# Interleaving softmax tiles and banded-weight reads with the normalise, write and transpose steps of a windowed-attention layer on eight cores

## What is computed

```python
xn = layernorm(x)
w = softmax(einsum('btc,fc->btf', xn, w_lin).reshape(B, T, H, K))   # 31 weights per row and head
# banded weights: row t of head h uses rows t-30 .. t of xn
out = einsum('bhts,bhsr->bhtr', banded(w), heads(xn))
x = x + out
w_ternary = where(w > d, 1, where(w < -d, -1, 0))   # d = 0.7 * mean(|weight|)
x = x + layernorm(x) @ (w_ternary * alpha).T + bias
```

## Time and profile before

| | |
|---|---|
| device time, median of 2 runs | 425.77 us (417.42 and 434.12) |
| the profiled execution, device time | 420.13 us |
| its span on the slowest core (core 7) | 418.6 us |
| spans of the eight cores | 406.2 to 418.6 us |
| busy: PE, DVE, ACT | 41%, 32%, 17% |
| mean DMA rate | 154 GB/s |

### The profile page before, as it was taken

One profiled execution on the slowest core, in us unless ns is written; L12 is line 12 of the kernel. 1 busy time (PEld: TensorE's weight loads), 2 busy tenths in 40 slices (PEclk: granted clock), 3 DMA queues, 4 the chain that ended last, 5 costly groups with the idle time before them and its releaser, 6 DMA issues.

```text
span 418.6 us, 2990 instructions; the slowest of 8 cores (406.2 to 418.6 us)
## 1 busy us (share of the span) xinstructions
PE 170.6 (41%) x940; PEld 94.6 (23%) x940; DVE 131.9 (32%) x250; ACT 69.7 (17%) x78; POOL 5.8 (1%) x8
## 2 busy tenths in 40 slices
PE   0000304000522532547579059530000499299990
PEld 0000001000200110114578059430000133033330
DVE  1462985200220220222585327460000022222321
ACT  0007045918010111011100000005650000000000
POOL 5000000000000000000000000000000000000000
PEclk9999856655656756676655555555555599689996
DMA  7999931089998996443699999602227676733422
GB/s 230 283 255 313 341 80 33 1 205 223 296 141 164 201 150 179 100 100 75 152 203 163 141 246 174 109 0 100 100 100 164 101 96 101 198 145 138 165 100 101
DMA packets 85544, 64.53 MB, mean 154 GB/s; under 512 B 69008, under 2 KB 70032, under 8 KB 85528
## 3 DMA queue, kind: packets, MB, share of 16 engines
q10 hardware_dynamic: 33136, 48.31, 43.9%
q1 hardware_dynamic: 51288, 15.01, 23.6%
q0 software_dynamic: 1104, 1.02, 1.9%
HBM read 23.14 MB, written 25.40 MB: 116 GB/s over the span
## 4 chain that ended last, share of the span: by engine, by line
DMA 33%; ACTq 14%; PE 14%; DVE 10%; ACT 9%; SPq 9%; DVEq 4%; issue 4%; POOLq 1%
DMA stage<-wpad 15%; ACTq L555 10%; SPq L199 9%; DMA wlTb<-wlT 8%; DMA wet<-stage 4%; DMA xn2d<-xn2r 3%; PE ps_at L618 3%; ACT xn L497 3%; ACT xn2r L536 2%; PE ps_ff L641 2%; PE ps_ff L643 2%; DVEq L337 2%; PE ps_wp L641 2%; PE ps_wp L643 2%; DVE redt L300 2%
## 5 line engine op out<-in xcount | busy, mean ns | idle before, releaser
L591 PE MATMUL ps_wp<-wlTb,xn1T 128*128 128x496 bf16 x128 | 45.1, 532 | 97.6 <-ACT wpad L457 85.0
L618 PE MATMUL ps_at<-wins,wet 128*64 128x64 bf16 x512 | 50.8, 305 | 28.8 <-DMA wet<-stage 21.5
L618 PEld LDWEIGHTS ps_at<-wins,wet 128*64 128x64 bf16 x512 | 50.2, 216 | 29.7 <-issue 29.7
L641 PE MATMUL ps_ff<-wtern,xn2T 128*128 128x512 bf16 x64 | 27.4, 428 | 61.7 <-DMA xn2T<-xn2d 53.7
L591 PEld LDWEIGHTS ps_wp<-wlTb,xn1T 128*128 128x128 bf16 x128 | 16.1, 131 | 126.1 <-issue 123.0
L335 DVE TENSOR_REDUCE sumc<-wpad 128x16 f32<-128x496 bf16 x16 | 10.7, 666 | 84.7 <-ACT wpad L457 84.7
L382 DVE TENSOR_TENSOR outst<-ps_ff,xs 128x512 f32<-128x512 f32 x16 | 10.3, 686 | 72.4 <-PE ps_ff L645 55.6
L345 DVE TENSOR_TENSOR xs<-ps_at,xs 128x1024 f32<-128x1024 f32 x16 | 19.6, 1223 | 29.3 <-PE ps_at L618 29.3
L643 PE MATMUL ps_ff<-wtern,xn2T 128*128 128x512 bf16 x64 | 27.2, 425 | 0.0
L137 DVE BATCH_NORM_STATS2 statsw<-xs 128x6 f32<-128x512 f32 x32 | 22.0, 688 | 15.7 <-DMA xs<-x 14.1
L536 ACT ACTIVATE xn2r<-xs,scn,scr 128x1024 bf16<-128x1024 f32 x16 | 18.5, 1228 | 38.8 <-DVEq L368 25.9
(11 more groups left out here) (83 smaller groups left out, 95.1 us busy)
## 6 DMA issues: line engine op xcount, KB each, us to landing
stage<-wpad ACTq DMA_DIRECT2D x16, 512.2 KB, 7.1
wins<-xn1d ACTq DMA_DIRECT2D x16, 512.0 KB, 10.9
out<-outst ACTq DMA_DIRECT2D x8, 1024.0 KB, 4.1
wTf<-wT ACTq DMA_DIRECT2D x1, 4096.0 KB, 38.0
xs<-x ACTq DMA_DIRECT2D x1, 4096.0 KB, 49.3
xn2d<-xn2r ACTq DMA_DIRECT2D x4, 1024.0 KB, 4.6
xn1d<-xn ACTq DMA_DIRECT2D x3, 1024.0 KB, 8.6
xs<-x ACTq DMA_DIRECT2D x2, 1024.0 KB, 10.7
```

Of the source, the lines that this page charges most:

```text
L591: mm = tensor.matmul(pw[:, 0:F], xn1T[:, cc * T + i * 128:cc * T + (i + 1) * 128], wlTb[:, cc * F:(cc + 1) * F], start=(cc == 0), stop=(cc ...
L618: mm = tensor.matmul(pa[64 * jj:64 * jj + 64, h * R:(h + 1) * R], lhsT, rhs, start=True, stop=True)
L641: tensor.matmul(fb[0][:], lhs, wtern[:, cc * C:cc * C + 512], start=(cc == 0), stop=False)
```

## The change

SP no longer issues all four groups of transposes before the first wet read: it issues wet 0 after T0, wet 1 after T1, wet 2 after T2, and wet 3 to 7 after T3. ScalarE runs `exp_act(i-4)` after it has normalised tile i, and the stage write after every second one; the exponentials 12 to 15 follow behind. The scales of tiles 8 to 15 are made before tile 5 and not before tile 8, and the window reads stand behind the exponential and stage write of that step. VectorE adds the sign tiles before it takes the statistics of tiles 8 to 15. The projection uses four PSUM banks in turn and not two, so tile i waits for the exponential of tile i-4.

```diff
-            for b in range(n_wb):
+                if q_ < 3 and q_ < n_wb:
+                    wet_xbar(q_)
+            for b in range(3 if n_wb > 3 else n_wb, n_wb):
                 wet_xbar(b)
...
-        vector.wait_ge(sems["ldx2"], 16)
-        for i in range(8, NT):
-            stats_tile(vector, xs[:, i * C:i * C + 512], xs[:, i * C + 512:(i + 1) * C], 1 + i, 128)
-        stats_batch(vector, 9, 17, scm1[:, 9:17], scv1[:, 9:17], scq1[:, 9:17], scn1[:, 9:17])
-        vector.drain().then_inc(sems["ln1s"], 1)
         for q in range(8):
             vector.wait_ge(sems["tch"], q + 1)
...
                                  ALU.add).then_inc(sems["tern"], 1)
+        vector.wait_ge(sems["ldx2"], 16)
+        for i in range(8, NT):
+            stats_tile(vector, xs[:, i * C:i * C + 512], xs[:, i * C + 512:(i + 1) * C], 1 + i, 128)
+        stats_batch(vector, 9, 17, scm1[:, 9:17], scv1[:, 9:17], scq1[:, 9:17], scn1[:, 9:17])
+        vector.drain().then_inc(sems["ln1s"], 1)
...
+        wpbanks_s = [ps_wp[0], ps_wp[1], ps_ff[0], ps_ff[1]]
...
-            inap = bass.AP(ps_wp[i % 2], 0, [[512, 128], [K, H], [1, K]])
+            inap = bass.AP(wpbanks_s[i % 4], 0, [[512, 128], [K, H], [1, K]])
...
         for i in range(4, NT):
-            if i == 8:
+            if i == 5:
                 scalar.wait_ge(sems["ln1s"], 2)
...
                 scalar.drain().then_inc(sems["rinv1"], 1)
+            if i == 8:
                 scalar.wait_ge(sems["cols1"], 2)
...
+            if level >= 2:
+                j = i - 4
+                exp_act(j)
+                if level >= 3 and j % 2 == 1:
+                    stage_wr(j // 2)
+            if level >= 2 and i % 4 == 3:
+                w = i // 4
                 while nextp < 5 and 128 * nextp + 258 <= 32 + 512 * (w + 1):
                     win_read(nextp)
                     nextp += 1
         if level >= 2:
-            for j in range(NT):
+            for j in range(12, NT):
                 exp_act(j)
...
+        wpbanks = [ps_wp[0], ps_wp[1], ps_ff[0], ps_ff[1]]
...
-            if i >= 2:
-                tensor.wait_ge(sems["expd"], i - 1)
-            pw = ps_wp[i % 2]
+            if i >= 4:
+                tensor.wait_ge(sems["expd"], i - 3)
+            pw = wpbanks[i % 4]
```

## The result

The changed kernel takes 440.07 us (median of 11 runs, 436.71 to 447.94), the kernel before 423.62 (median of 10). The ratio is 1.047, with a 95% interval of 1.041 to 1.053: slower by 4.7%. Some executions of every kernel are disturbed and run a few per cent longer, so ratios here are taken over the undisturbed ones alone (hence 1.047 and not 440.07 / 423.62 = 1.039) and are missing where there were too few, medians are taken over all, and the traces of three kernels (VectorE's new order alone, groups ahead, early windows), being of disturbed executions, are only an indication. The profiled execution of the changed kernel took 438.33 us, its slowest core (core 6) a span of 436.6.

A forecast was written before the change was run, and what follows sets the result against it. No engine was taken to bound the kernel, but a ring of exponential, division, stage write and landing. An earlier start lost to three round trips put exp 12 18.6 us later: 420.1 + 18.6 = 438.7, so 439, range 425 to 456.

The forecast's parts named there:

- the ring: Loop of exp, norm, stage write, landing, exp, as `wpad` holds one pair; three of seven beats grow from 12 to 16 us.
- The prologue gains: Before the pair loop: ScalarE's 8.53 us wait for sign tiles goes; first stage write's issues end 20 us earlier, near 89.5.
- First long beat: Exp 2 to exp 4: group write, T1 and first projection tile join the beat, 32.8 us; exp 4 at 129.3.
- The other two windows: Exp 4 to 8 and 8 to 12: a normal beat plus a long one, 39.6 us each, before 29.9 and 23.6.
- Exp 12: Exponential of tile 12, whose shift is taken as the end's: at 208.5, 18.6 us later than before.
- SP's order costs nothing and the earlier wet 0 to 2 gain nothing: SP's queue: interleaving costs only traffic; earlier wet 0 to 2 gain nothing, since wet 3 to 7 end last.
- Four banks gain 0: Projection: TensorE may run up to two more tiles ahead, but into the same ring, so gains 0.
- The end follows exp 12: Aggregation and tail: the same code remains behind exp 12, so the end shifts with it, 18.6 us.
- The early start is kept: Rival: group round trips under the ring's beat, so the 20 us earlier start reaches the end, 400; with faster transposes 0.07.
- Cancel: Rival: transfers in the ring run as if alone, exp 12 only 3.1 us later, end 423; chance 0.16.
- Collision: Rival: traffic collides in each window, exp 12 at 236, up to 46 us later, taken as 452; chance 0.17.
- What would show it: Signs in the trace: exp 1 near 86, TensorE waiting for `xn1T`, ScalarE's stage-write wait about 50, alternating gaps between exponentials.

The follow-up runs named there:

- groups ahead: Changed kernel with ScalarE normalising and writing each group of four tiles ahead of its four exponentials: 428.39 us, 1.013 against the kernel before; with SP's old order 414.78, 0.985.
- early windows: ScalarE works during stage landings, SP issues window reads 0 to 2 behind T0 and wet reads one group later: 420.21 us, before 429.72, no ratio.

## Why the prediction was right

Forecast 439, measured 440.07 (and 438.33 for the profiled execution). The mechanism, three round trips in the ring, is what the runs show; that the sum came this close is in part luck, as the terms show. By its own steps:

- **The prologue gains.** Right to a few tenths. Exp 0 at 72.69 (72.4), statistics 72.36 to 84.1 (72.1 to 84.0), exp 1 at 86.17 (86.2), second issue of stage write 0 at 89.64 (89.5), exp 2 at 96.23 (96.5).
- **First long beat.** 37.5 us for 32.8, exp 4 at 133.7 for 129.3. The term that was mis-sized is the group write beside wet 0: 13.35 for 8.5, above the 9.5 that I had as its most. T1 at 18.3 (forecast 19) was right.
- **The other two windows.** 37.7 and 37.0 for 39.6. The normal beat was 13.1 and 12.6 (14.0), since a wet read alone lands in 6 us and is gone before the stage write; the group write 4.40 and 4.21 (7.8), below the 7.1 that I had as its least; T2 and T3 both 14.3 (12.5); the tile 3.5 to 3.7 (3.3).
- **Exp 12** at 208.41 for 208.5. These errors, +4.4, -1.9 and -2.6, cancel by luck: the sum is better than its terms. Over the eight cores exp 14 moved by 17.0 in the mean (199.7 to 216.6).
- **SP's order costs nothing and the earlier wet 0 to 2 gain nothing.** This step failed. In the changed kernel the old order is slower (1.079 against 1.047, 10 us at exp 14). It didn't hurt the sum, since the forecast compares with the kernel before, where those reads ran at 137 to 166 us, ahead of the last beats too; but the argument, that only wet 3 to 7 end last, overlooked where wet 0 to 2 would run otherwise: beside the last beats. And wet 0, which I had costed as a little traffic, is what trebled the first group write: without wet 0 it took 4.23 and had landed before the window reads began, and with wet 0 but no window reads it took 9.53 (on another core).
- **Four banks gain 0.** Right within what was measured.
- **The end follows exp 12.** Exp 12 +18.6, exp 14 +19.2, span +18.0. Right. The wet reads' tail is the same picture shifted:

```profile
233.28 17.35 SPq L199
250.82 12.89 SPq L199
263.95 5.91 SPq L199
270.51 17.01 DMA wet<-stage
287.96 6.52 PE ps_at L632 x64
```

  Before, its first long issue began at 214.08.
- **The rivals.** "The early start is kept" is refuted by the chain. "Cancel" assumed transfers as if alone: later group writes were even quicker than its 7.1, but T1 and the first write were not alone, and T2 and T3 took 14.3, not 11.9. "Collision" holds for the first long beat alone (36.8, measured 37.5).
- **What would show it.** Waits of TensorE for `xn1T` before tiles 4, 8 and 12: yes. ScalarE's wait for stage writes was to be about 50, a figure without a sum, and is 23.9: four waits of 4.67, 5.02, 4.93 and 9.31, the first three shortened by a normalise that runs meanwhile. Gaps of 33, 14, 26, 14, 26: measured 37.5, 13.1, 24.5, 12.6, 24.4.

T2 and T3 moved 1.05 MB each in 14.3 us, 73 GB/s; eight issues of about 1.26 us at the least are 10 of it. The rate of the Trainium skill (DMA: Bandwidth & Descriptors, Latency and other measured facts), by which the end would have been at an estimated 408, doesn't hold here, nor for a wet read with little beside it (1.05 MB in 6.3 us, 167 GB/s).

Beyond my own account: the theory that a decoupled order gives 30 us and more was right in sign and wrong in size. With the groups ahead the medians are 12 us below the changed kernel (forecast 30 to 38) and, with SP's old order, 25 below it (forecast 40 to 48); that is 1.5% better than the kernel before, not 5 to 7. Before the change the DMA engines were busy 83% of the phase, so 22 us of idle time were left. What the change loses is overlap. Why so little of the 22 us can be had is argued and not shown: in the traces of the reordered kernels the beat stretches with what is put beside it.

## What to carry to other kernels

When an interleaving moves a producer (normalise, write, transpose) between the waits of a ring, ask which of its results the next turn of the ring needs: its whole round trip is then a term of the beat, here 24 us twice and some 37 once, for a first stage write that is 20 us earlier. Issue the producer of the next group ahead of the wait, not behind it. And before expecting much from more overlap, multiply the idle share of the DMA engines by the phase's length (here 22 us of 130 before): it is a rough ceiling, since the busy time itself changes with the order (97, 103, 108 and 116 us in four kernels here).

## What was not expected of the hardware

**A transfer's time depends strongly on its company.** A wet read of 1.05 MB landed in 15.0 us before, also in the changed kernel as wet 0, and wet 1 in 6.3 with only the end of T1 beside it. From the list of DMA issues of the changed kernel, in stretches of a microsecond or so, wet 0, the group write beside it, wet 1 and the next group write (us from issue to landing at the end):

```profile
wet<-stage SPq DMA_TRANSPOSE x1, 15.0
...
xn1d<-xn ACTq DMA_DIRECT2D x1, 1024.0 KB, 13.4
...
wet<-stage SPq DMA_TRANSPOSE x1, 6.3
...
xn1d<-xn ACTq DMA_DIRECT2D x1, 1024.0 KB, 4.4
```

A group write of 1 MB is 4.4 alone and 13.4 beside a wet read, a stage write and window reads. Eight transposes are 12.1 to 14.3 us with little beside, 25.4 and 29.6 beside five window reads. The quiet figures can't be read from a kernel that keeps its DMA engines busy, which is why my least and most for the group write were both wrong.

**The cores fall into two groups.** In the changed kernel cores 0, 3, 4 and 6 reach exp 14 at 219.7 to 222.3 and cores 1, 2, 5 and 7 at 211.8 to 213.7: one of each pair 0 and 1, 2 and 3, 4 and 5, 6 and 7. The split arises at wet 0 and the first group write. Core 7 had, for the same two transfers:

```profile
xn1d<-xn ACTq DMA_DIRECT2D x1, 1024.0 KB, 7.2
...
wet<-stage SPq DMA_TRANSPOSE x1, 9.3
```

against 13.4 and 15.0 on core 6. The changed kernel with two banks has the same split, again one core of each pair, but not the same ones (cores 0, 3, 5 and 7 at 220.4 to 220.9, the others at 211.5 to 214.1), so it isn't a matter of which core. With SP's old order in the changed kernel, where wet 0 doesn't run beside the group write, exp 4 comes at 130.4 to 131.7 on all eight cores and the split is gone. That the cores of a pair compete for something, and one wins, would fit; no run here tests it, and the kernel before does not show so clean a split (exp 14 at 195.5 to 203.6).
